# A token tower with routed experts: turned logits in the outputs' bank, gelu split from rounding, halves in the order 1, 0, and other orders on three engines

## What is computed

```python
H = jax.nn.gelu(xf @ W1 + b1, approximate=False)          # 64 -> 256
probs = jax.nn.softmax((H @ Wg + bg) / TEMP, axis=-1)      # 8 experts
assign = jnp.argmax(probs, axis=-1)
out = jnp.zeros_like(xf)
for e in range(Wd.shape[0]):
    y = H @ Wd[e] + bd[e]
    sel = (assign == e)[:, None]
    out = out + jnp.where(sel, probs[:, e:e + 1] * y, 0.0)
```

## Time and profile before

| | us |
|---|---|
| median of 3 timed runs | 124.19 |
| lowest, highest of them | 121.47, 128.94 |
| the profiled execution | 120.68 |
| its span, first to last instruction | 118.9 |
| TensorE matmul busy | 100.9 (85%) |
| VectorE busy | 91.1 (77%) |
| ScalarE busy | 68.8 (58%) |
| GpSimd busy | 55.8 (47%) |

### The profile page before, as it was taken

The page is one execution under the profiler, slowest core; times in us unless marked ns, Lnnn a source line. Parts: engine busy times, 40 slices in busy tenths (PEclk is TensorE's granted clock), DMA queues, the critical chain, the costliest instruction groups (busy, mean ns, idle before and its releaser), DMA issues.

```text
span 118.9 us, 1851 instructions
## 1 busy us (share of the span) xinstructions
PE 100.9 (85%) x649; PEld 72.0 (61%) x651; DVE 91.1 (77%) x229; ACT 68.8 (58%) x117; POOL 55.8 (47%) x101
## 2 busy tenths in 40 slices
PE   5740999988799999999989899879498998999940
PEld 1240777418532799968879587656286565676620
DVE  0347999999999998899963999792943965377981
ACT  2803568949999999989944376334810840634000
POOL 7599899889994006125188051655005000000580
PEclk9999999999557999558999999999999999999999
DMA  4999800000000000000000000000000000000033
GB/s 117 238 195 378 338 3 6 0 0 0 0 0 0 6 3 3 0 0 0 0 6 0 0 0 0 0 6 0 3 0 0 0 0 0 6 0 0 0 88 88
DMA packets 3449, 4.40 MB, mean 37 GB/s; under 512 B 2288, under 2 KB 2544, under 8 KB 3312
## 3 DMA queue, kind: packets, MB, share of 16 engines
q1 hardware_dynamic: 3136, 3.91, 11.1%
q10 hardware_dynamic: 304, 0.38, 1.5%
HBM read 3.76 MB, written 0.52 MB: 36 GB/s over the span
## 4 chain that ended last, share of the span: by engine, by line
PE 56%; DVE 14%; ACT 13%; DMA 7%; POOL 4%; issue 3%; SPq 0%; POOLq 0%
PE pair L1022 16%; PE pair L915 10%; PE pair L901 8%; DMA ids<-x 7%; PE pair L949 7%; ACT angle L494 3%; ACT bell L454 3%; PE bank L986 3%; DVE pair L776 3%; PE pair L1029 3%; PE hid_pair L938 2%; DVE wave L744 2%; PE hid_pair L998 2%; ACT wave L460 2%; POOL rstd L377 2%
## 5 line engine op out<-in xcount | busy, mean ns | idle before, releaser
L371 POOL TENSOR_SCALAR var_eps<-mean_var 128x4 f32<-128x4 f32 x8 | 3.3, 408 | 29.9 <-DVE mean_var L712 29.6
L776 DVE COPY_PREDICATED pair<-later,pair 128x256 f32<-128x256 int32 (+3 forms) x30 | 12.3, 410 | 5.9 <-PE pair L1022 5.1
L949 PEld LDWEIGHTS pair<-amps,bell 128*128 128x128 f32 x128 | 15.9, 202 | 0.5 <-issue 0.3
L949 PE MATMUL pair<-amps,bell 128*128 128x64 f32 x128 | 15.7, 284 | 0.0
L901 PE MATMUL pair<-onehot,w1p 128*128 128x512 f32 x32 | 9.9, 478 | 3.0 <-DVE w1p L615 3.0
L501 ACT ACTIVATE bell<-hid_pair,sm 128x512 f32<-128x512 f32 x8 | 5.1, 683 | 12.3 <-PE hid_pair L998 12.3
L915 PE MATMUL pair<-h,w_sb 128*64 128x512 f32 x40 | 11.7, 743 | 0.0
L387 POOL TENSOR_TENSOR angle<-picked,prob 128x256 f32<-128x256 f32 x3 | 1.8, 613 | 20.1 <-DVE prob L800 20.1
L697 DVE SCALAR_TENSOR_TENSOR bell<-bell,scale_w,wave 128x512 f32<-128x512 f32 x16 | 11.1, 758 | 0.0
L1022 PE MATMUL pair<-wd_high,H_high 128*128 128x512 f32 x32 | 10.8, 419 | 0.0
L901 PEld LDWEIGHTS pair<-onehot,w1p 128*128 128x128 f32 x32 | 7.5, 240 | 5.0 <-DVE w1p L615 3.1
(11 more groups left out here) (160 smaller groups left out, 226.2 us busy)
## 6 DMA issues: line engine op xcount, KB each, us to landing
ids<-x SPq DMA_DIRECT2D x2, 512.0 KB, 6.8
posb<-positions SPq DMA_DIRECT2D x1, 768.0 KB, 9.8
wd_sb<-wd SPq DMA_DIRECT2D x1, 512.0 KB, 10.9
out<-angle SPq DMA_DIRECT2D x4, 128.0 KB, 2.0
st_sb<-state SPq DMA_DIRECT2D x1, 328.0 KB, 10.1
bd_sb<-bd ACTq DMA_DIRECT2D x2, 128.0 KB, 7.9
w_sb<-w SPq DMA_DIRECT2D x1, 256.0 KB, 8.4
posb<-positions SPq DMA_DIRECT2D x1, 256.0 KB, 8.4
```

Of the source, the lines that this page charges most:

```text
L776: return dve.copy_predicated(held[:, :, 0:n, 0, 0:D], repeat(later[:, g, 2 * h + rows.start:2 * h + rows.stop, first:first + n], 3, D), he ...
L949: mm = pe.matmul(bank[g][:, b * D:(b + 1) * D], bell[:, g, at:at + P], amps[:, g * GB + b, :], start=(s == 0), stop=(s == NS - 1))
```

## The change

- The transposed logits move from bank 6, beside the gate rows, to columns 256 to 383 of bank 5, which holds the state layer's outputs. TensorE's `hidden(g)` waits for the copy of gate rows g-1 (`s_gcopy`) and no longer for the reading of the logits. `logits_back(g, added)` waits also until `added` residuals are added and until the logits before are read; `outputs(3, 1)` waits until logits 0 are read.
- On ScalarE, rounding is a call of its own, `round_hidden(g)`, with other calls between it and the gelu: `normalise(1, 2)` for group 1, `gate_out(2)` and `transposed_out(1, 3)` for group 2; `normalise(1, 3)` goes ahead of `hidden(2)`.
- On VectorE, `route(0)` goes behind `turn_back(3)`, and `residual(3)`, `moments(1, 3)` behind `pick(0, 1)` and ahead of `pick(0, 0)`. Half 1 is picked ahead of half 0 in every group, in the last one too.
- On TensorE, half 1 goes ahead of half 0, and from the first experts on the list is another: `experts_high(0, 0)` stands ahead of `turn(1, 1)`; `outputs(3)` and `gate(1)` stand ahead of `turn(1, 2)`; `logits_back(g)` stands later; `hidden(g + 1)` stands ahead of the logits and of one half of the high part.

The diff, without its last lines of context (the functions are as printed above where no line is marked):

```diff
-        logit_cols = bank[6][:, P:2 * P].rearrange("p (j e) -> p j e", e=GATE)
+        logit_cols = layer_bank[:, 2 * P:3 * P].rearrange("p (j e) -> p j e", e=GATE)
...
+            def round_hidden(g):
+
                 if g > 1:
                     for h in range(2):
                         act.wait_ge(s_exp_mm[h], g - 1)
...
             hidden(0)
+            round_hidden(0)
             normalise(0, 3)
...
             normalise(1, 2)
+            round_hidden(1)
             transposed_out(1, 2)
             gate_out(1)
+            normalise(1, 3)
             hidden(2)
-            normalise(1, 3)
+            gate_out(2)
             transposed_out(1, 3)
-            gate_out(2)
+            round_hidden(2)
             hidden(3)
+            round_hidden(3)
             gate_out(3)
...
-                dve.wait_ge(s_last_mm, 2 * h + jj + 1)
+                dve.wait_ge(s_last_mm, 2 * (1 - h) + jj + 1)
...
             split_hidden(0)
-            route(0)
             residual(2)
             driven(3)
             moments(1, 2)
             scan(3)
             turn_back(3)
+            route(0)
+            pick(0, 1)
+            residual(3)
+            moments(1, 3)
             pick(0, 0)
             split_hidden(1)
-            residual(3)
-            moments(1, 3)
             route(1)
-            pick(0, 1)
+            pick(1, 1)
+            split_hidden(2)
             pick(1, 0)
-            split_hidden(2)
-            pick(1, 1)
             route(2)
-            pick(2, 0)
+            pick(2, 1)
             split_hidden(3)
             route(3)
             softmax_in()
-            pick(2, 1)
+            pick(2, 0)
             probability()
             dve.wait_ge(s_prob, 1)
-            for h in range(2):
+            for h in (1, 0):
...
-            def outputs(g):
+            def outputs(g, routed=0):
...
+                if routed:
+                    pe.wait_ge(s_lread, routed)
...
             def hidden(g):
                 pe.wait_ge(s_xT[1], g + 1)
                 if g:
-                    pe.wait_ge(s_lread, g)
-
+                    pe.wait_ge(s_gcopy, g)
...
-            def logits_back(g):
+            def logits_back(g, added):
 
                 pe.wait_ge(s_gcopy, g + 1)
+                pe.wait_ge(s_hb, added)
+                if g:
+                    pe.wait_ge(s_lread, g)
...
             experts_high(0, 1)
-            logits_back(0)
             turn(0, 3)
             outputs(2)
             inputs_in(3)
+            logits_back(0, 3)
+            experts_high(0, 0)
             turn(1, 1)
-            experts_high(0, 0)
+            experts_low(0, 1)
             hidden(1)
             experts_low(0, 0)
-            experts_low(0, 1)
+            outputs(3, 1)
+            gate(1)
             turn(1, 2)
-            outputs(3)
-            gate(1)
+            experts_high(1, 1)
+            hidden(2)
+            logits_back(1, 4)
             experts_high(1, 0)
-            logits_back(1)
-            hidden(2)
-            experts_low(1, 0)
-            experts_high(1, 1)
+            gate(2)
             turn(1, 3)
             experts_low(1, 1)
-            gate(2)
-            experts_high(2, 0)
-            logits_back(2)
             hidden(3)
-            experts_low(2, 0)
+            experts_low(1, 0)
+            logits_back(2, 4)
             experts_high(2, 1)
             gate(3)
             experts_low(2, 1)
-            logits_back(3)
-            for h in range(2):
+            experts_high(2, 0)
+            logits_back(3, 4)
+            experts_low(2, 0)
+            for h in (1, 0):
                 experts_high(3, h)
                 experts_low(3, h)
```

## The result

| | before | changed |
|---|---|---|
| median of the timed runs, us | 122.92 (4 runs, 121.47 to 128.94) | 117.17 (4 runs, 116.27 to 117.33) |
| ratio | | 0.963, 95% interval 0.956 to 0.971 |
| the profiled execution, us | 120.68 | 116.27 |
| its span, us | 118.9 | 114.5 |
| TensorE's stretch, from the start of `turn(0, 3)` to its last matmul's end, us | 73.65 to 114.33, 40.68 | 73.47 to 109.91, 36.44 |

The time fell by 3.7%. Of the 4.4 us of span, 4.24 lie in one stretch of TensorE, 0.11 in the transpose of logits 0 that no longer stands ahead of it, and under 0.1 us in the stages before. Two more executions of the changed kernel, not among the four of the table, took 117.47 and 119.85 us.

What follows compares the result with a forecast made beforehand. TensorE's program order, with five stops summing to 3.81 us, was taken to bound the stretch from 73.5 us on; 3.8 us off the 124.19 us median gave 120.4 us, range 116.4 to 125.0.

Steps and rivals of the forecast that it cites:

- The bound and the mechanism: TensorE's order bounds the stretch from 73.5 us; all five stops go, gain 3.8 us, tail stays 4.6 us; chance 0.62.
- The signs named for this case: For: no TensorE stop over 0.2 us, last expert matmul 110 to 110.6. Against: waits over 0.5 us, or VectorE later.
- The walk: TensorE's new list from 73.54 us, written as starts from block lengths: end at 110.0 us, 4.3 us before 114.33.
- The size, 3.8 us: Sum of TensorE's five stops, 1.24, 1.68, twice 0.38 and 0.13 us, together 3.81; the walk's 4.3 was the upper bound.
- The bank move: Turned logits in bank 5: removes the stops of 0.38 us before `hidden(2)` and `hidden(3)`; two added waits cost nothing.
- The gain of 0.13 us for the halves' order: Order 1, 0 gives `experts_high(1, 1)` the half whose pick was made first, so its 0.13 us stop goes.
- The gelu's split: On ScalarE, `normalise(1, 2)` between gelu and rounding: gives nothing by itself, makes covering the stop before `turn(1, 2)` possible.
- The tight hand-overs: Places where TensorE nearly waits for ScalarE's or VectorE's results: every spare positive in the walk, 0.3 to 1.0 us.
- GpSimd: Group 3's chain beside VectorE's pick and split: might take 3.53 instead of 1.82 us, delaying gate(2) 1.2 us, gain 2.6.
- A part coming back as new waits: Rival: waits at the tight hand-overs, above all gate(2), leave a gain of 1.6 to 2.6 us; chance 0.24.
- VectorE setting the pace: Rival: idle time moves to the end because VectorE's picks set the pace; gain about 0 to 1 us; chance 0.08.
- The clock rival: Rival: TensorE's clock falls within the expert stage, making the kernel slower, 127 us; chance 0.06.

Runs made afterwards that it cites:

- The two undone orders: Changed kernel with `turn(1, 1)` ahead of `experts_high(0, 0)` again, stretch 37.87 us; or `turn(1, 2)` ahead of `outputs(3, 1)` and `gate(1)` again, 38.15 us in its second profile.
- two experiments with a stop of 1.55 and 2.33 us: Changed kernel with `turn(1, 2)` ahead of `outputs(3, 1)` and `gate(1)`, stretch 41.12 us; or with halves 0, 1 from group 1 on, 40.47 us.
- The version with parts and two stores: Changed kernel with the last half computed part by part and the last group's result stored in two DMAs: median 117.26 us, ratio 0.956.

## Why the prediction was right

**The bound and the mechanism.** Right. TensorE's order bound the stretch, all five stops went, none came back, the tail stayed at 4.6 us, and the clock stayed at 1.0 in the stage. The signs named for this case are in the profile, but for one missed by a hair (the last expert matmul ends at 109.91 us, not at 110 to 110.6), and none of those against it.

**The walk.** Its starts hold within 0.4 us throughout, and within 0.15 from high(1,0) at 88.8 us on: turn(1,1) 79.1 forecast, 78.91 measured; turn(1,2) 85.0 and 84.64; gate(2) 91.3 and 91.27; high(2,1) 95.5 and 95.43; high(3,0) 106.6 and 106.47; end 110.0 and 109.91. Adding blocks of known length, start to start, was the exact way, though part of the last 0.1 us is luck: at turn(1,2) the walk was 0.36 us late, and seams that it left out took most of that back up to gate(2).

**The size, 3.8 us.** Here a term was mis-sized: the stretch lost 4.24 us. I took the sum of the brackets and called the walk's 4.3 an upper bound. A bracket counts from the modelled end of the matmul before, but the next one could have started ahead of that end. Measured start to start, the stops were 1.41 (inputs take 0.91, 75.43 to 76.34 in the changed kernel, so the turn could have begun at 76.51), 1.76 (of the eight low matmuls from 81.82 on, four take 1.03, as at 81.21 in the changed kernel, and four 1.00, as at 105.47), 0.53 and 0.54 (logits 0.11 from 90.67, then `hidden`), and 0.30 us: 4.54 in place of 3.81. Of that 0.30 us went back into seams: the four transposes of logits cost 0.70 us in their new places. Before, the three that lie in the stretch cost 0.42, and the first lay ahead of it. That is 0.28 of the 0.30 us. The two undone orders confirm the larger figures: 1.43 and 1.71 us of stretch for stops whose brackets read 1.22 and 1.56.

**Parts.** The bank move was put at nothing lost and two stops won; alone it gives 0.49 us, because one of the two turns into a wait for a pick. The gain of 0.13 us for the halves' order was its smallest use: in the new order of TensorE, taking it away costs a stop of 2.33 us. The prediction did say that `experts_high(1, 1)` has the half picked first, but did not price what the other order would do. The gelu's split was put at nothing by itself and as what makes the cover possible; undone, it costs 0.38 us.

**The tight hand-overs.** Their spare time, forecast and measured, in us: gate(2) behind gelu 2, 0.5 and 0.6; high(1,1) behind rounding 1, 0.3 and 0.5; high(2,1) behind pick(1,1), 0.5 and 0.3; high(1,0) behind pick(0,0), 1.0 and 1.45; high(3,0) behind pick(2,0), 0.9 and 0.7. The rows of ScalarE and VectorE:

```profile
82.48 1.43 ACT L494 ACTIVATE angle<-h_b,offset,rstd 128x64 f32<-128x64 f32 x4
83.80 1.13 ACT L512 CAST H_high<-bell 128x512 fp32r<-128x512 f32 x2
...
89.39 1.24 ACT L501 ACTIVATE bell<-hid_pair,sm 128x512 f32<-128x512 f32 x2
```

```profile
87.06 0.29 DVE L793 COPY picked<-pair 128x128 f32<-128x128 f32 x1
...
94.84 0.29 DVE L793 COPY picked<-pair 128x128 f32<-128x128 f32 x1
...
105.50 0.29 DVE L793 COPY picked<-pair 128x128 f32<-128x128 f32 x1
```

**GpSimd.** For group 3 its chain took 2.28 us, between the 1.82 and the 3.53 of the earlier trace rows, and only its last instruction was held up:

```profile
85.73 0.23 POOL L371 TENSOR_SCALAR var_eps<-mean_var 128x4 f32<-128x4 f32 x1 [3.96 <-DVE mean_var L719]
...
87.35 0.66 POOL L378 TENSOR_TENSOR offset<-negated,rstd 128x4 f32<-128x4 f32 x1
```

While VectorE picked (85.56 to 87.03) the chain ran at its old pace; when `split_hidden(1)` began at 87.27, the instruction issued beside it took 0.66 us instead of 0.20. The Trainium skill (SBUF — State Buffer, "Who interferes with whom") says that a VectorE instruction with two SBUF inputs contends with a GpSimd instruction that reads SBUF, and that one with at most one SBUF input, outside the two-port modes, does not. This trace agrees: the split reads `bell` and `H_high`, both in SBUF, the pick reads `pair` in PSUM and only the mask in SBUF. It cost TensorE nothing.

**The rivals.** A part coming back as new waits, and VectorE setting the pace, did not happen. The clock rival did not happen to the changed kernel, but is real on this stretch: two experiments with a stop of 1.55 and 2.33 us lost 3.0 and 1.6 us behind it. I had argued from the kernel before keeping its clock through 1.24 and 1.68 us; one profile did not show that this can be relied on. Its price was read too low as well. The convolution's run of 7.08 us starts at 31.85 us and ends at 38.93, so not all of it lies in the two slices at half the clock, and 0.58 us for each microsecond of full-speed work is less than the half clock costs. In the profile of the stop of 1.55 us nearly 7 us at half the clock cost 2.97, about 0.77 us for each microsecond of full-speed work. (The clock line has full speed from the twentieth slice on, not from the nineteenth, which has 0.8; nothing hangs on it.)

**The number.** 120.4 us was the median of three timed runs less 3.8. The measured 117.17 us is less mostly because that median, 124.19, lay 3.5 us above the profiled execution of the kernel before; from this one the same sum gave 116.9, where 116.27 was measured. Of these 0.6 us, 0.4 are the mis-sized term and 0.1 the transpose of logits 0 that no longer stands ahead of the stretch. As a ratio the forecast was 0.969, inside the measured interval.

## What to carry to other kernels

When one engine works through a hand-written list without holes except for a few stops, write the new list out as starts, from block lengths taken start to start, and check each hand-over's spare time; that gave the end within 0.1 us. The idle time in brackets understates a stop of TensorE, by 0.1 to 0.2 us each here. Orders of two engines belong together: the half computed first must be the half picked first, and one swapped pair cost 2.4 us of stretch by its stop, and with the clock fall behind it as much as the whole change had gained.

## What the runs showed that I had not expected

- A stop of 1.55 us in a stretch of otherwise full work was followed in one execution by nearly 7 us at half the clock, worth 2.97 us, and in another execution of the same program by none. The changed kernel, with no stop in the stage, did not show it in its two profiles; of its twelve executions one, of 119.85 us and without a profile, lay over 2 us above all others.
- What starts such a fall stays open, and so does whether the stop has a part in it: stops of 1.22 and 1.68 us in the bank move's profile, and of 1.56 us in the second one of `turn(1, 2)` first, had none behind them. Filling the stop with idle matmuls left six of twelve executions high, so either the filling does not help, or the high ones come from falls elsewhere; in two profiles (a mean of 0.57 from 44 to 60 us, and of 0.72 from 58 to 74) they lay before the stretch. The version with parts and two stores has no stop at all in the stretch, and three of its six executions were long.
- The last store's size hardly matters to the end: stores of 64 KB took 1.8 us and stores of 128 KB 2.0 us, and splitting the last one won 0.05 us.
